# Attention sums turned and divided on VectorE by 32x32 transposes instead of on TensorE

## The reference

```python
def _attn(q, k, v, mask):                       # 16 heads of 8
    scores = jnp.einsum('bqhd,bkhd->bhqk', q, k) / np.float32(np.sqrt(HD))
    scores = jnp.where(mask[:, None, None, :], jnp.float32(-jnp.inf), scores)
    w = jax.nn.softmax(scores, axis=-1)
    return jnp.einsum('bhqk,bkhd->bqhd', w, v)
for i in range(NL):                             # 6 layers
    xn = _adaln(x, noise_emb, n1_w[i], n1_b[i])
    ...
    x = x + _attn(q, k, v, src_mask).reshape(B, L, D) @ so_w[i].T
    xn = _adaln(x, noise_emb, n2_w[i], n2_b[i])
    ...
    x = x + _attn(q, k, v, ctx_mask).reshape(B, L, D) @ co_w[i].T
    xn = _adaln(x, noise_emb, n3_w[i], n3_b[i])
    h = jax.nn.gelu(xn @ f1_w[i].T + f1_b[i], approximate=False)
    x = x + (h @ f2_w[i].T + f2_b[i])
```

## Time and profile before

| | |
|---|---|
| median of 3 runs | 2361.25 us (2357.6 to 2362.25) |
| profiled execution | span 2365.3 us from the first to the last instruction; no other time is given for it |
| TensorE busy | 2218.9 us, 94% of the span |
| VectorE busy | 1930.4 us, 82% |
| ScalarE busy | 1761.9 us, 74% |
| GpSimd busy | 1082.6 us, 46% |
| mean granted TensorE clock | 0.975 of full speed |

### The profile page before, as it was taken

How to read it: one execution, slowest core, us unless ns; L and a number is a source line. 1 busy time by engine, 2 the same in 40 slices (tenths; PEclk the granted TensorE clock), 3 DMA queues, 4 the chain that set the end, 5 groups by cost and what they waited for, 6 DMA issues and landing times.

```text
span 2365.3 us, 46233 instructions
## 1 busy us (share of the span) xinstructions
PE 2218.9 (94%) x17034; PEld 960.1 (41%) x17034; DVE 1930.4 (82%) x3983; ACT 1761.9 (74%) x3601; POOL 1082.6 (46%) x1348
## 2 busy tenths in 40 slices
PE   6999999999688999999999999999999999999979
PEld 3455455545322333333343333333343334333336
DVE  6778889698778888888888888898888888888435
ACT  4778778696166778788888787887888887777744
POOL 3656556466334434434444443533454444432324
PEclk9999999999589999999999999999999999999979
DMA  2000000000312211212222321212222322111000
GB/s 84 2 1 1 1 2 1 30 1 20 90 50 63 82 50 54 65 46 72 62 67 69 82 63 48 67 51 66 54 74 63 81 63 66 49 49 52 25 23 19
DMA packets 108570, 113.07 MB, mean 48 GB/s; under 512 B 15809, under 2 KB 96951, under 8 KB 107319
## 3 DMA queue, kind: packets, MB, share of 16 engines
q1 hardware_dynamic: 108345, 110.12, 17.1%
HBM read 14.80 MB, written 1.05 MB: 7 GB/s over the span
## 4 chain that ended last, share of the span: by engine, by line
PE 63%; DVE 14%; ACT 10%; DMA 4%; POOL 4%; issue 3%; SPq 2%; DVEq 0%; POOLq 0%; ACTq 0%
PE psum L1487 11%; PE psum L1455 6%; PE psum L1467 6%; DVE A L1977 5%; PE psum L1258 4%; PE psum L1599 4%; PE psum L1591 4%; PE psum L1559 3%; PE psum L1388 3%; PE psum L1342 3%; DMA A<-A 3%; ACT A L2137 3%; DVE A L1999 3%; PE psum L1548 2%; PE psum L1354 2%
## 5 line engine op out<-in xcount | busy, mean ns | idle before, releaser
L1977 DVE TENSOR_REDUCE A<-psum 128x1 f32<-128x512 f32 x1536 | 969.9, 682 | 141.5 <-PE psum L1467 133.4
L2197 ACT ACTIVATE A<-psum 128x512 f32<-128x512 f32 x1536 | 821.4, 604 | 206.0 <-PE psum L1455 177.9
L1467 PE MATMUL psum<-A 64*128 64x512 bf16 x1536 | 421.8, 391 | 35.9 <-DVE A L1977 12.8
L1455 PE MATMUL psum<-A 64*128 64x512 bf16 x1536 | 403.9, 384 | 15.6 <-DVE A L1977 6.0
L1487 PE MATMUL psum<-A 128*9 128x512 f32 (+1 forms) x3072 | 405.2, 604 | 1.6 <-ACT A L2197 1.5
L2342 POOL TENSOR_TENSOR A<-A,rden 128x512 f32<-128x512 f32 x256 | 266.7, 1067 | 177.5 <-DVE rden L1862 176.7
L2373 POOL TENSOR_TENSOR A<-A 128x512 f32<-128x512 f32 (+1 forms) x78 | 96.6, 1239 | 301.8 <-DMA A<-A 291.8
L1467 PEld LDWEIGHTS psum<-A 64*128 64x128 bf16 x1536 | 105.1, 94 | 309.7 <-DVE A L1977 116.7
L2227 ACT ACTIVATE A<-psum 77x512 f32<-77x512 f32 x384 | 199.7, 598 | 30.3 <-PE psum L1548 29.7
L1455 PEld LDWEIGHTS psum<-A 64*128 64x128 bf16 x1536 | 103.5, 94 | 277.2 <-DVE A L1977 103.8
L2137 ACT ACTIVATE A<-psum,nm 128x512 f32<-128x512 f32 x256 | 176.0, 688 | 45.0 <-DVE nm L1850 44.1
(11 more groups left out here) (209 smaller groups left out, 3743.4 us busy)
## 6 DMA issues: line engine op xcount, KB each, us to landing
A<-A SPq DMA_DIRECT2D x456, 128.0 KB, 2.4
A<-A SPq DMA_DIRECT2D x336, 64.0 KB, 2.0
A<-zero SPq DMA_DIRECT2D x51, 128.0 KB, 2.4
wl<-in_wl SPq DMA_DIRECT2D x6, 1024.0 KB, 5.8
A<-A SPq DMA_DIRECT2D x36, 78.0 KB, 2.1
A<-in_nT SPq DMA_DIRECT2D x1, 1664.0 KB, 6.8
A<-in_w SPq DMA_DIRECT2D x2, 512.0 KB, 7.0
A<-in_w SPq DMA_DIRECT2D x1, 1024.0 KB, 6.1
```

What stands on the lines that cost most here:

```text
L1455: handle.matmul(bank(b), k_st[bt][lo:lo + ROW, h // 2, k * P:(k + 1) * P], q_st[m % 3][lo:lo + ROW, h // 2, :], start=True, stop=True).the ...
L1467: handle.matmul(bank(b), q_st[m % 3][lo:lo + ROW, pair, q * P:(q + 1) * P], k_st[bt][lo:lo + ROW, pair, :], start=True, stop=True).then_in ...
L1977: handle.tensor_reduce(nm[:, pair // 4, q, j, pair % 4:pair % 4 + 1], bank(BANKS["maximum"][i]), AX.X, ALU.max, negate=True).then_inc(mx, 1)
L2197: handle.activation(pT[:, block % 2, i % GROUP, :], bank(BANKS["scores"][i]), ACT.Exp, scale=HD1 ** -0.5).then_inc(ex, 1)
```

## The change

Per half, VectorE itself turns the bank of sums with its transpose, which works within blocks of 32 partitions by 32 columns: `o_flip` reads bank 5 and writes SBUF. A quadrant of 32 partitions holds two heads with 18 rows; afterwards these are 18 columns in a block of 50, where the second half puts its 18 behind the first's (its other columns are not used). On the 128 partitions then stand tokens modulo 32, one quadrant for each group of heads, and in a block the four heads of 9 columns. `o_invert` takes all 64 reciprocals of a partition at once, `o_divide` multiplies in place (512 columns), and `o_back` flips back into `attT_s`, from which `so` reads. The cross attention has `co_flip`, `co_invert`, `co_divide`, `co_back` and an `attT_c` of its own. `o_turn`, `att_turn`, `co_turn`, `catt_turn` and the six ScalarE copies are gone, and so are their banks; a bank of sums is now freed by the flip. Per step: 24 transposes, 6 copies and 8 VectorE instructions out, 10 VectorE instructions in.

The other parts keep their order, and all banks stay. The new parts' places in VectorE's order: co_flip 0 between max 63 and max 0; co_flip 1 behind max 7, then max 8, co_invert, max 9, co_divide, co_back, max 10, o_flip 0; and cross_max 4, o_flip 1, max 39, o_invert, max 40, o_divide, max 41, o_back, cross_max 5. PLACED_ tables are written anew to keep single steps' orders.

Two waits are new beside these: `exp` 4 of step 0 waits for the 18 DMAs of zeros and masks, and the statistics of the first part (`moments`) wait for their own engine's last use of the same buffer.

```diff
@@ -248,14 +248,17 @@
         xnT_s = A0[:, A_LAST:A_LAST + S]
         assert taken[0] <= A_LIVE
         taken[0] = A_LIVE
-        o_s = words(S)
-        att_s = words(S).rearrange("p (q c) -> p q c", q=QT)
+        FLIP = 2 * HW * HALVES + 32 - 2 * HW
+
+        def flipped():
+
+            return words(S // 32 * FLIP).rearrange("p (b r) -> p b r", r=FLIP)
+
+        o_s, attT_s = flipped(), words(S)
         tcq = Turned()
         y_s, y_c, y_f = (w.t1.rearrange("p (q c) -> p q c", q=QT) for w in (tq, tcq, tk))
         xnT_c, xnT_f = words(S), words(S)
-        o_c = words(S)
-        att_c = words(S).rearrange("p (q c) -> p q c", q=QT)
-        attT = words(S)
+        o_c, attT_c = flipped(), words(S)
         st_c, mv_c, ve_c, rs_c = step_norm()
         st_f, mv_f, ve_f, rs_f = step_norm()
         cnm = words(64).rearrange("p (q j u) -> p q j u", q=QT, j=2)
@@ -263,8 +266,9 @@
         cnmb_raw = words(256)
         cnmb = cnmb_raw.bitcast(bf16).rearrange("p (q c) -> p q c", q=QT)
         cnmT = tcq.lo
+        rd_c = words(64).rearrange("p (b x) -> p b x", x=2 * HALVES)
         assert taken[0] <= A_NORMS
-        rd = words(64).rearrange("p (h x s) -> p h x s", h=HALVES, s=2)
+        rd_s = words(64).rearrange("p (b x) -> p b x", x=2 * HALVES)
 
         wm = wl[:, 0, 0:1552]
         wgT = wm[:, 0:512]
...
         VECTOR = {
...
-            "cdivide": [193, 206],
-            "divide": [40, 78],
...
+            "co_flip": [203, 216],
+            "co_invert": 218,
+            "co_divide": 220,
+            "co_back": 221,
+            "o_flip": [31, 69],
+            "o_invert": 71,
+            "o_divide": 73,
+            "o_back": 75,
...
@@ -1440,7 +1438,7 @@
                     owner[b] = (b_x, bt + 1)
 
 
-            def out_project(w, b):
+            def out_project(attT, w, b):
                 for q in range(QT):
                     t = handle.matmul(psum[:, b, q * P:(q + 1) * P], attT[:, q * P:(q + 1) * P], w, start=True, stop=True)
                 return t
@@ -1488,23 +1486,11 @@
                                           start=k == 0, stop=k == QT - 1)
                     t.then_inc(pv_ps, 1)
                     owner[b] = (o_sb, HALVES * m + g // 2 + 1)
-                if name == "o_turn":
-                    b = BANKS["o_turn"][i]
-                    pe.wait_ge(o_sb, HALVES * m + i + 1)
-                    free(b)
-                    turn4(b, four(o_s)).then_inc(ob_ps, 1)
-                    owner[b] = (att, HALVES * m + i + 1)
-                if name == "att_turn":
-                    b = BANKS["att_turn"][0]
-                    pe.wait_ge(att, HALVES * (m + 1))
-                    free(b)
-                    turn4(b, att_s).then_inc(sa_ps, 1)
-                    owner[b] = (sa_T, m + 1)
                 if name == "so":
                     b = BANKS["so"][0]
-                    pe.wait_ge(sa_T, m + 1)
-                    free(b)
-                    out_project(wcols(m, W_SO, D), b).then_inc(so_ps, 1)
+                    pe.wait_ge(att, m + 1)
+                    free(b)
+                    out_project(attT_s, wcols(m, W_SO, D), b).then_inc(so_ps, 1)
                     owner[b] = (x_so, m + 1)
                 if name == "c_turn":
                     b = BANKS["c_turn"][0]
@@ -1560,23 +1546,11 @@
                                           start=True, stop=True)
                     t.then_inc(cpv_ps, 1)
                     owner[b] = (co_sb, HALVES * m + i // 2 + 1)
-                if name == "co_turn":
-                    b = BANKS["co_turn"][i]
-                    pe.wait_ge(co_sb, HALVES * m + i + 1)
-                    free(b)
-                    turn4(b, four(o_c)).then_inc(cob_ps, 1)
-                    owner[b] = (catt, HALVES * m + i + 1)
-                if name == "catt_turn":
-                    b = BANKS["catt_turn"][0]
-                    pe.wait_ge(catt, HALVES * (m + 1))
-                    free(b)
-                    turn4(b, att_c).then_inc(ca_ps, 1)
-                    owner[b] = (ca_T, m + 1)
                 if name == "co":
                     b = BANKS["co"][0]
-                    pe.wait_ge(ca_T, m + 1)
-                    free(b)
-                    out_project(wcols(m, W_CO, D), b).then_inc(co_ps, 1)
+                    pe.wait_ge(catt, m + 1)
+                    free(b)
+                    out_project(attT_c, wcols(m, W_CO, D), b).then_inc(co_ps, 1)
                     owner[b] = (x_co, m + 1)
                 if name == "f_turn":
                     b = BANKS["f_turn"][0]
@@ -1701,7 +1675,10 @@
             def after_own():
                 dve.wait_ge(d_own, own.n)
 
+            summed = {}
+
             def moments(src, st, mv, n, rows):
+                dve.wait_ge(d_own, summed.get(id(st), 0))
                 for q in range(n):
                     t = handle.bn_stats(st[0:rows, q, :], src[0:rows, q, :])
                 t.then_inc(own.next(), 1)
@@ -1709,6 +1686,7 @@
                 for q in range(n):
                     t = handle.bn_aggr(mv[0:rows, q, :], st[0:rows, q, :])
                 t.then_inc(own.next(), 1)
+                summed[id(st)] = own.n
                 after_own()
 
             def variance(src, chain, n, rows):
@@ -1946,15 +1924,26 @@
                 t.then_inc(own.next(), 1)
 
 
-            def divide(b, half, attended):
-
-                o = bank(b).rearrange("p (x r) -> p x r", r=32)[:, :, 0:2 * HW].rearrange("p x (s d) -> p x s d", d=HW)
-                handle.reciprocal(rd[:, half, :, :], o[:, :, :, HD1]).then_inc(own.next(), 1)
-                after_own()
-                n = 2 * HD1
-                dst = attended.rearrange("p q (j r) -> p (q j) r", j=GROUP)[:, :, half * n:(half + 1) * n]
-                return handle.tensor_tensor(dst.rearrange("p x (s d) -> p x s d", d=HD1), o[:, :, :, 0:HD1],
-                                            rd[:, half, :, :].unsqueeze(3).to_broadcast([P, QT * GROUP, 2, HD1]), ALU.mult)
+            def flip(b, half, o):
+
+                return handle.transpose(o[:, :, 2 * HW * half:2 * HW * half + 32], bank(b).rearrange("p (b q) -> p b q", q=32))
+
+            def of_heads(o):
+
+                return o[:, :, 0:2 * HW * HALVES].rearrange("p b (x d) -> p b x d", d=HW)
+
+            def invert(o, rd):
+
+                return handle.reciprocal(rd, of_heads(o)[:, :, :, HD1])
+
+            def divide(o, rd):
+
+                rows = of_heads(o)[:, :, :, 0:HD1]
+                return handle.tensor_tensor(rows, rows, rd.unsqueeze(3).to_broadcast([P, S // 32, 2 * HALVES, HD1]), ALU.mult)
+
+            def flip_back(o, attT):
+
+                return handle.transpose(attT.rearrange("p (b x d) -> p b x d", x=2 * HALVES, d=HD1), of_heads(o)[:, :, :, 0:HD1])
 
             def statistics(m, st, mv, ready, value):
 
@@ -1975,11 +1964,21 @@
                         dve.wait_ge(sh, 2 * (m - 1) + pair // 4 + 1)
                     dve.wait_ge(mx_ps, 64 * m + i + 1)
                     handle.tensor_reduce(nm[:, pair // 4, q, j, pair % 4:pair % 4 + 1], bank(BANKS["maximum"][i]), AX.X, ALU.max, negate=True).then_inc(mx, 1)
-                if name == "divide":
-                    dve.wait_ge(ob_ps, HALVES * m + i + 1)
-                    dve.wait_ge(sa_ps, m)
-                    dve.wait_ge(b_h, 5 * B)
-                    divide(BANKS["o_turn"][i], i, att_s).then_inc(att, 1)
+                if name == "o_flip":
+                    dve.wait_ge(pv_ps, 16 * m + 8 * i + 8)
+                    dve.wait_ge(b_w, B)
+                    dve.wait_ge(*((o_sb, HALVES * m + 1) if i else (att, m)))
+                    flip(BANKS["weigh"][i], i, o_s).then_inc(o_sb, 1)
+                if name == "o_invert":
+                    dve.wait_ge(o_sb, HALVES * (m + 1))
+                    invert(o_s, rd_s).then_inc(own.next(), 1)
+                if name == "o_divide":
+                    after_own()
+                    divide(o_s, rd_s).then_inc(own.next(), 1)
+                if name == "o_back":
+                    after_own()
+                    dve.wait_ge(so_ps, m)
+                    flip_back(o_s, attT_s).then_inc(att, 1)
                 if name == "x_so":
                     dve.wait_ge(so_ps, m + 1)
                     handle.tensor_tensor(x1(m), x1(m), four(bank(one("so"))), ALU.add).then_inc(x_so, 1)
```

More of the change, by code:

```diff
@@ new lines, in build @@
+                        ("max", 9, 21): [("co_divide", 0, 18)],
+                        ("cross_max", 1, 19): [("max", 34, 21)],
+                        ("cross_max", 2, 19): [("x_f", 0, 18), ("max", 37, 21)],
+                        ("max", 38, 21): [("s_stats", 0, 22)],
+                        ("o_flip", 1, 20): [("max", 39, 21)],
+                        ("o_invert", 0, 20): [("max", 40, 21)],
+                        ("o_divide", 0, 20): [("max", 41, 21)],
+                        ("o_back", 0, 20): [("cross_max", 5, 19)],
```

1324 lines of the change are left out of this document (649 added, 675 removed), and 8 rows, old and new, of the table PLACED_POOL.

## The result

The changed kernel takes 2522.85 us (median; 2520.2 to 2527.42), the kernel before 2361.75 beside it: a ratio of 1.068 (95% interval 1.065 to 1.070). Predicted were 2402 us, in a range from 2325 to 2435: the direction was right, the size was not, +161 us instead of +41. The profiled execution of after has a span of 2518.4 us. One execution among all runs of this document, in the kernel with one added reduction, took 4000 us where its nine others took 2377 to 2388; its ratio is without it.

The account below looks back on a forecast made before the run. VectorE was taken to bound S3, TensorE and VectorE both to fill S1, TensorE the rest. +2.2 us a pass in 21 passes (+46), +3 for two earlier passes and -8 at the end made +41: 2402 us, range 2325 to 2435.

Parts of the forecast that it names:

- What bounds the kernel: One pass cut in five stretches: VectorE bounds S3, S1 is full on TensorE and VectorE, the chain elsewhere runs over TensorE.
- S3: Stretch from the f2 update to cross maximum 5: four added VectorE parts lie straight on the chain, +2.4 us a pass.
- S1: Stretch from first maximum to f1: VectorE gets 1.0 us longer, less 0.2 of room, +0.8 us a pass.
- R1: Rival: VectorE absorbs its added 1.0 us in S1, so TensorE keeps its 2.3 saved; 2337 us, chance 0.18.
- R2: Rival: TensorE is the bound everywhere, its 94% busy share read literally; -81 us, 2280 us, chance 0.07.
- R3: Rival: a VectorE transpose goes through twice, 0.6 us more for five of six flips; 2465 us, chance 0.08.
- R4: Rival: low-end prices, flips at 0.35 us and cheaper reciprocals; 2366 us, no change, chance 0.07.
- S2: Stretch with f1, GELU and f2 following each other; VectorE's later end fits its idle time, 0 us.
- The clock: Sign of a wrong prediction: the clock falls, each TensorE piece at half clock costing double; no price in the sum.
- S4: Stretch from cross maximum 5 to qk_rope 0: TensorE saves the group of transposes o_turn 1, -0.58 us a pass.
- S5: Stretch from qk_rope 0 to maximum 0: TensorE saves att_turn, -0.44 us; co_flip 0 falls into VectorE's idle time.
- The end, -8: Last three steps, cross parts after the last maximum: removed turns and copies give way to VectorE work, 2.7 us saved a step.

Follow-up runs that it names:

- the filled waits: The changed kernel with useless transposes on TensorE where it waits for VectorE, in steps 2 to 17; 2473.8 us, ratio 1.045.
- no division: The changed kernel without its reciprocals and multiplies (o_invert, o_divide, co_invert, co_divide), leaving out the softmax's denominators; 2411.4 us, ratio 1.019.

## Why the prediction was wrong

- *What bounds the kernel*: right. S3 is VectorE's, S1 is full on both; R1 and R2, which had TensorE's gain reach the end, are refuted. R3 too (0.71, not 1.2), and R4: the flips were not cheap.
- *S3, +2.4*: right, +2.2 measured; the chain from the update through cross maximum 5 is 11.1 us long, 11.3 were named.
- *S2, 0*: right. VectorE's two waits there are as they were, 1.26 and 2.27.
- *The clock*: this step failed. The prediction named a falling clock as what would make it wrong and gave it no price, since the passes of before had 1.00 and the only row at a low level was in the ramp. But my own steps said that TensorE would sit idle: 2.4 us more in S3, and its 2.3 saved "go into waiting for banks" in S1. I priced the waits and not what follows them: 3.0 to 3.1 us a pass by the filled waits, 49 us in the 16 passes that were filled, an estimated 65 over 21. It is the largest part of the miss.
- *S1, +0.8*: mis-sized beside the clock. With the waits filled the stretch with S1 and S2 is 2.3 us longer than in before. 0.6 of it is the multiply, taken at 0.75 because "what stretches the others the rows don't say". The trace of before did say it. Of the twelve L1724 of the earlier trace rows the nine of 0.69 us stand alone and the three of 1.41 began while a GpSimd instruction ran, and so did another of that line:

```profile
2322.88 1.64 DVE L1724 TENSOR_TENSOR x_st<-x_st,rstd 128x512 f32<-128x512 f32 x1
```

```profile
2322.33 1.64 POOL L2434 TENSOR_TENSOR A<-A 128x512 f32<-128x512 f32 x1 [8.85 <-DVE A L2087]
```

  VectorE's other added work is the 1.0 of my sum. The last 0.7 to 0.8 is idle time of VectorE, waiting for TensorE (4.75 us a pass in this stretch instead of 3.98), where the sum had 0.2 of room to take up; how much of it is the filling's own is not told apart.
- *S4, -0.58*: failed, and not only for the clock. Where the clock is kept the stretch from cross maximum 5 to qk_rope 0 takes 7.2 us (waits filled) and 7.03 (no division), and 7.06 in before. TensorE saves o_turn 1, but then waits 0.38 us for ScalarE, which makes the operand of the next matmuls (L1614 in before, L1588 in after) from s_turn. In before the turn stood in that place and there was no wait. Before, then after:

```profile
1251.27 0.66 PE L1258 MATMUL psum<-ident,A 128*128 128x128 f32 x4
1251.76 1.08 PE L1614 MATMUL psum<-A,wl 128*128 128x512 f32 x2
```

```profile
1229.74 1.13 PE L1588 MATMUL psum<-A,wl 128*128 128x512 f32 x2 [0.38 <-ACT A L2198]
```

- *S5, -0.44*: failed. Its mean is the same to 0.04 us. In the pass shown TensorE is done earlier and waits for the DMA; the way through SP, GpSimd and the DMAs is as long as before, and I had followed no chain beside the one that ended last. In passes where TensorE does not wait maximum 0 comes 17.68 us behind qk_rope 0 and 17.73 in before; why TensorE's own part saves so little there was not followed up.
- *The end, -8*: not tested by a run of its own. The last two distances between f2 updates are 48.1 and 40.0 in after, 45.7 and 42.6 in before, so no large gain or loss lies there.

Added up for a mean pass: 2.23 for S3, 3.04 for the clock, 0.59 for the multiply, 1.71 for the rest of S1, 0.14 in S4 and 0.04 in S5 are the 7.75 measured, where the sum had 2.2. They close because each part is a difference between means of kernels with one edit between them; what two causes do together stands with the one that was taken away first. So the sum was 5.5 us a pass too small, 116 us in 21 passes, nearly all of the 120 us that it missed.

## What to carry to other kernels

Where a change makes TensorE wait longer, even below two microseconds at a time, look up its granted clock behind the longest waits, and price the work behind a new wait at both levels: 0.6 us of new VectorE work cost 0.6, the next 0.6 cost 1.3, and the same work in VectorE's idle time cost a tenth of that. Moving work off the busiest engine gives nothing where that work filled a wait for another engine, and where a stretch gets shorter by the sum, follow the second chain through it (here over SP, GpSimd and a DMA, and in S4 over ScalarE) before you count the gain. Compare means over the passes, not one pass with another.

## What was not expected of the hardware

- The clock fell to 0.50 with no single wait of TensorE over 1.71 us in S1 and 1.20 in S3 in the pass shown; it was busy 1.40 and 1.81 of 4 us there. The same wait of 1.51 us had the lower clock behind it in one pass and not in the next.
- Useless transposes in the waits made the kernel 49 us faster.
- VectorE's 32x32 transpose of 128x512 in fp32 costs the same from PSUM and from SBUF, 705 and 707 ns, and the same as a copy of that size (683).
